# Three buffers for the driven input of a selective scan, and each chunk's gate made by VectorE straight from PSUM

## The reference

```
dA[t]  = exp(delta[t] * A[s])
dBu[t] = (delta[t] * u[t]) * B[t, s]
h[t]   = dA[t] * h[t-1] + dBu[t]              # a scan over the 1024 tokens
y[t]  += h[t] * C[t, s]                       # summed over the 16 states
y = (y + u * D) * silu(z)                     # the gate
attn = y @ Wout.T + bout
```

## Time and profile before

| | |
|---|---|
| median of 3 timed runs | 860.98 us (860.31, 860.98, 864.2) |
| span of the profiled execution, first to last instruction | 858.1 us |
| scan stage in it, first drive to last back | 131.7 to 556.4 us |
| PE, DVE, ACT, POOL busy over the span | 84, 75, 38, 60% |

### The profile page before, as it was taken

The page is one execution under the profiler, slowest core; times in us unless marked ns, Lnnn a source line. Parts: engine busy times, 40 slices in busy tenths (PEclk is TensorE's granted clock), DMA queues, the critical chain, the costliest instruction groups (busy, mean ns, idle before and its releaser), DMA issues.

```text
span 858.1 us, 10173 instructions
## 1 busy us (share of the span) xinstructions
PE 723.1 (84%) x2245; PEld 358.4 (42%) x2246; DVE 646.2 (75%) x880; ACT 328.8 (38%) x364; POOL 512.9 (60%) x266
## 2 busy tenths in 40 slices
PE   6899998778787777878788787996599999999994
PEld 3444343223232222323233232585356666666663
DVE  5388898999999999999999999677444444445442
ACT  1786956455453544444454453111111111111110
POOL 1013234989989899998999999646622222222222
PEclk9999999999999999999999999997599999999998
DMA  9345635766777686586669897297323312322210
GB/s 290 104 138 159 213 140 147 204 171 162 180 175 191 164 199 180 146 207 152 190 174 248 219 223 219 67 386 259 115 74 62 49 33 45 48 42 42 46 29 0
DMA packets 61731, 126.33 MB, mean 147 GB/s; under 512 B 11338, under 2 KB 33290, under 8 KB 61580
## 3 DMA queue, kind: packets, MB, share of 16 engines
q1 hardware_dynamic: 49908, 116.12, 49.5%
q0 software_dynamic: 7152, 8.48, 5.7%
q10 hardware_dynamic: 4648, 1.48, 0.7%
HBM read 98.08 MB, written 24.69 MB: 143 GB/s over the span
## 4 chain that ended last, share of the span: by engine, by line
PE 40%; DVE 28%; issue 13%; POOL 9%; ACT 6%; DMA 1%; DVEq 0%; ACTq 0%; SPq 0%; POOLq 0%
DVE pool L1166 19%; PE PS L740 16%; PE PS L756 8%; POOL pool L1449 6%; PE PS L513 6%; ACT PS L906 5%; PE PS L618 4%; POOL spread L1469 2%; PE PS L748 2%; DVE pool L1154 2%; PE PS L636 2%; DVE pool L1100 1%; DVE pool L1098 1%; PE PS L600 1%; DVE Y L1109 1%
## 5 line engine op out<-in xcount | busy, mean ns | idle before, releaser
L1449 POOL TENSOR_TENSOR pool<-pool,hT 128x1024 f32<-128x1024 f32 x128 | 298.6, 2357 | 24.6 <-PE PS L618 24.6
L618 PE MATMUL PS<-pool,ident 128*128 128x512 f32 x512 | 249.5, 610 | 33.9 <-POOL pool L1449 32.6
L906 ACT ACTIVATE PS<-pool,negA 128x1024 f32 (+1 forms) x128 | 143.1, 1118 | 192.1 <-DVE pool L1166 192.1
L1166 DVE TENSOR_TENSOR_SCAN pool<-PS,pool 128x1024 f32<-128x1024 f32 x96 | 215.7, 2274 | 0.0
L1519 POOL DMA_INDIRECT out<-uT,ptab x39 | 60.5, 1552 | 168.7 <-DVE uT L1395 162.1
L618 PEld LDWEIGHTS PS<-pool,ident 128*128 128x128 f32 x512 | 94.0, 192 | 134.8 <-issue 71.1
L740 PE MATMUL PS<-pool,uT 128*128 (+1 forms) x312 | 145.1, 609 | 0.0
L1154 DVE TENSOR_TENSOR pool<-PS,pool 128x1024 f32<-128x1024 f32 x96 | 117.6, 1225 | 12.5 <-PE PS L600 2.4
L600 PE MATMUL PS<-pool 96*128 96x512 bf16 x256 | 78.8, 390 | 56.2 <-DVE pool L1154 52.9
L1369 DVE TENSOR_TENSOR uT<-uT,PS 128x512 f32<-128x512 f32 x39 | 26.9, 688 | 88.3 <-PE PS L740 85.5
L1469 POOL TENSOR_TENSOR spread<-spread,pool 128x1024 f32<-128x1024 f32 x32 | 75.4, 2357 | 14.9 <-ACT spread L912 14.9
(11 more groups left out here) (174 smaller groups left out, 726.6 us busy)
## 6 DMA issues: line engine op xcount, KB each, us to landing
hT<-C_scratch SPq DMA_DIRECT2D x128, 512.0 KB, 5.3
pool<-in_w SPq DMA_DIRECT2D x16, 512.0 KB
uT<-expert_in_scratch SPq DMA_DIRECT2D x39, 130.5 KB
Y<-Y SPq DMA_DIRECT2D x32, 128.0 KB, 2.4
C_scratch<-Y SPq DMA_DIRECT2D x8, 512.0 KB, 2.6
pool<-du_scratch SPq DMA_DIRECT2D x8, 512.0 KB, 7.2
Y<-in_wo SPq DMA_DIRECT2D x8, 512.0 KB
expert_in_scratch<-zrow SPq DMA_DIRECT2D x16, 130.5 KB, 5.8
```

What stands on the lines that cost most here:

```text
L618: m = pe.matmul(PS[:, 6 + half, :], ident[:, :], prod[:, k % PR, HF * half:HF * half + HF], start=False, stop=k == DS - 1)
L906: act.activation(pair(2 * (k % 2)).unsqueeze(1), delta[:, bass.ds(g2 * 2 + r, 1), :], ACT.Exp, scale=decay[:, bass.ds(g2 * (2 * DS) + n, 1 ...
L1166: dve.tensor_tensor_scan(hst[:, k % HR, :], pair(2 * (k % 2)), driven, 0.0, ALU.mult, ALU.add).then_inc(scan_done, 1)
L1449: gp.tensor_tensor(prod[:, k % PR, :], hst[:, k % HR, :], crep[k % RC], ALU.mult).then_inc(prod_done, 1)
```

## The change

1. A third buffer for `drive`. It is `wz_sb`, the weights of z, which are free once z is made. The buffers are taken in turn by three, and the wait asks for one scan less: for the scans up to n-3, not for the one just before.
2. `leave` moves from ACT to DVE. It is now one multiplication, of the sum in PSUM (banks 6 and 7) by `szT`, written into `uT`: copy and gate in one. It stands behind `drive(4)` and ahead of `scan(3)` of the next chunk. It still signals `yev_done`, on which PE begins the next sum.
3. POOL's `gate_y` goes, and the semaphore `gated` with it; who waited for `gated` now waits for `yev_done`.
4. The last chunk leaves where DVE's last gate stood. Since that now reads the PSUM banks, PE's first gate logits wait for it.
5. As the first chunk has nothing that leaves, DVE's first pass of the loop is written out, and POOL's no longer is.

```
+        dbu_of = [dbu[:, 0, :], dbu[:, 1, :], wz_sb[:, :, :].rearrange("p k n -> p (k n)")]
...
-            sp.wait_ge(gated, NG)
+            sp.wait_ge(yev_done, 1 + NG)
...
-                    pe.wait_ge(gated, CH)
+                    pe.wait_ge(yev_done, 1 + CH)
...
             def logits(t):
                 pe.wait_ge(h2_done, t + 1)
+                if t == 0:
+                    pe.wait_ge(yev_done, 1 + NG)
...
-            def leave(g2, r):
-                act.wait_ge(ysum_done, g2 * (2 * DS) + ((r + 1) * DS + RC))
-                act.sem_inc(passed, 1)
-                act.activation(uT[:, bass.ds(g2 * 2 + r, 1), :], pair(6).unsqueeze(1),
-                               ACT.Copy).then_inc(yev_done, 1)
...
-                        if k == LAG - 1 and not (first and r == 0):
-                            leave(g2 - (1 - r), 1 - r)
...
-                dve.wait_ge(scan_done, g2 * (2 * DS) + (n + 1))
-                dve.tensor_tensor(dbu[:, owned_to(k) % 2, :], pair(4), du[:, r, :], ALU.mult).then_inc(dbu_done, 1)
+                dve.wait_ge(scan_done, g2 * (2 * DS) + n)
+                dve.tensor_tensor(dbu_of[owned_to(k) % 3], pair(4), du[:, r, :], ALU.mult).then_inc(dbu_done, 1)
...
+            def leave(g2, r):
+                chunk = bass.ds(g2 * 2 + r, 1)
+                dve.wait_ge(ysum_done, g2 * (2 * DS) + ((r + 1) * DS + RC))
+                dve.tensor_tensor(uT[:, chunk, :], pair(6).unsqueeze(1), szT[:, chunk, :], ALU.mult).then_inc(yev_done, 1)
...
                     for k in range(1, DS):
                         if k not in SHARED:
                             drive(g2, r, k)
+                        if k == LAG and not (first and r == 0):
+                            leave(g2 - (1 - r), 1 - r)
                         scan(g2, r, k - 1)
...
-            def gate_y(g2, r):
-                chunk = bass.ds(g2 * 2 + r, 1)
-                gp.wait_ge(yev_done, g2 * 2 + (r + 2))
-                gp.sem_inc(passed, 1)
-                gp.tensor_tensor(uT[:, chunk, :], uT[:, chunk, :], szT[:, chunk, :], ALU.mult).then_inc(gated, 1)
...
-                        if k == RC + 2 and not (first and r == 0):
-                            gate_y(g2 - (1 - r), 1 - r)
```

More of the change, by code:

```diff
@@ L246, in adaln_mamba_moe @@
         d_done, zero_rows, xs_zeroed, z_mm, sz_done = (sem(n) for n in ("d_done", "zero_rows", "xs_zeroed", "z_mm", "sz_done"))
-        folded, gated, bout_done = (sem(n) for n in ("folded", "gated", "bout_done"))
+        folded, bout_done = (sem(n) for n in ("folded", "bout_done"))
         regated = sem("regated")
@@ L631, in outward_y @@
                 if t == NTB:
-                    pe.wait_ge(gated, CH * NB)
+                    pe.wait_ge(yev_done, 1 + CH * NB)
                 if t >= 6:
@@ L955, in _ @@
                 decays_of(g2, False)
-            leave(NG // 2 - 1, 1)
             def take_h2(t):
@@ L1162, in scan @@
                 else:
-                    driven = dbu[:, owned_to(k) % 2, :]
+                    driven = dbu_of[owned_to(k) % 3]
                     dve.wait_ge(dbu_done, g2 * (2 * OWN) + (r * OWN + owned_to(k) + 2))
@@ L1167, in scan, with driven_of @@
                                        ALU.mult, ALU.add).then_inc(scan_done, 1)
-            def driven_of(g2, last):
+            def leave(g2, r):
+                chunk = bass.ds(g2 * 2 + r, 1)
+                dve.wait_ge(ysum_done, g2 * (2 * DS) + ((r + 1) * DS + RC))
+                dve.tensor_tensor(uT[:, chunk, :], pair(6).unsqueeze(1), szT[:, chunk, :], ALU.mult).then_inc(yev_done, 1)
+            def driven_of(g2, first, last):
                 for r in range(2):
@@ L1179, in _ @@
             drive(0, 0, 0)
-            with dve.Fori(0, NG // 2 - 1) as g2:
-                driven_of(g2, False)
-            driven_of(NG // 2 - 1, True)
+            driven_of(0, True, False)
+            with dve.Fori(1, NG // 2 - 1) as g2:
+                driven_of(g2, False, False)
+            driven_of(NG // 2 - 1, False, True)
             route = [0]
@@ L1285, in place_of, with leave_last @@
                     dve.tensor_copy(ready[:, :], late).then_inc(ready_known, 1)
-            def gate_y(c):
-                dve.wait_ge(yev_done, 1 + c + 1)
-                dve.tensor_tensor(uT[:, c, :], uT[:, c, :], szT[:, c, :], ALU.mult).then_inc(gated, 1)
+            def leave_last():
+                leave(NG // 2 - 1, 1)
             def residual(q):
@@ L1311, in _ @@
             normal_h2(0)
-            gate_y(NG - 1)
+            leave_last()
             for t in (TQ, TQ + 1):
@@ L1449, in weigh, with weighed_of @@
                 gp.tensor_tensor(prod[:, k % PR, :], hst[:, k % HR, :], crep[k % RC], ALU.mult).then_inc(prod_done, 1)
-            def gate_y(g2, r):
-                chunk = bass.ds(g2 * 2 + r, 1)
-                gp.wait_ge(yev_done, g2 * 2 + (r + 2))
-                gp.sem_inc(passed, 1)
-                gp.tensor_tensor(uT[:, chunk, :], uT[:, chunk, :], szT[:, chunk, :], ALU.mult).then_inc(gated, 1)
-            def weighed_of(g2, first):
+            def weighed_of(g2):
                 for r in range(2):
@@ L1471, in _ @@
             gp.sem_inc(ysum_done, RC)
-            weighed_of(0, True)
-            with gp.Fori(1, NG // 2) as g2:
-                weighed_of(g2, False)
+            with gp.Fori(0, NG // 2) as g2:
+                weighed_of(g2)
             def rstd_of(q):
```

## The result

The changed kernel takes 887.95 us (887.02 to 891.52), the kernel before 860.75 us in the runs beside it: ratio 1.0313, 95% interval 1.0282 to 1.0343. It is slower, as forecast, but by 27.2 us and not 12.9, and the time lies above the range. The span of its profiled execution is 884.9 us, 26.8 more than before.

The account below looks back on a forecast made before the run. VectorE (DVE) was taken to bound the scan stage, GpSimd (POOL) nearly full too. Terms -18.2 + 8.0 + 14.7 - 1.0 + 9.1 + 0.3 = +12.9 gave span 871.0, median 873.9 us; range 856 to 885.

Parts of the forecast that it names:

- Third buffer: Scan stage, VectorE: each of 96 drives starts 0.19 us earlier, no longer waiting for the scan just ahead: 18.2 us less.
- Gate on VectorE: Scan stage: seven `leave`s add a step of 1.14 us each to VectorE, 8.0 us more.
- The wait that it makes: Chunk boundaries: `leave` behind drive(4) delays TensorE, so VectorE idles 2.1 us before drive(5), seven times: 14.7 us more.
- GpSimd's part: Scan stage: GpSimd drops seven gates, 16.5 us beside VectorE; only 1.0 us less was counted, bounds 0 and 2.1.
- The clock: Chunk boundaries: TensorE's 3.9 us stop drops its clock at all seven, 1.3 us each: 9.1 us more, bounds 0 and 12.
- The sign: Whole kernel: slower than before, by 12.9 us in the sum; chance of slower beyond the 0.5% no-change band 0.65.
- Behind the scans: After the scan stage: TensorE's first logits wait for VectorE's last gate, 0.3 us more if it reaches the end.
- over 2 us in the experts' stage: Experts' stage: a move in time of more than 2 us there would show the prediction wrong altogether.
- Rival 1: Scan stage: the clock doesn't fall, or falls where nothing waits: 864.8 us, 52.1 us per chunk; chance 0.20.
- Rival 2: Chunk boundaries: the wait doesn't reach VectorE, as front(5) is ready when scan(3) ends: 848.7 us; chance 0.18.
- Rival 3: Scan stage: the third buffer buys nothing, the 0.10 us behind a scan isn't the semaphore: 890.7 us; chance 0.12.

Follow-up runs that it names:

- e6: Changed kernel with `leave` behind drive(3) instead of drive(4), and two drive buffers instead of three: 866.09 us, ratio 1.0058 to the kernel before.
- e4: Changed kernel with `leave` one step earlier on VectorE, behind drive(3) and ahead of scan(2): 848.31 us, ratio 0.9865 to the kernel before.
- e9: e3 plus a matmul of zeros ahead of each back but a chunk's first: 867.29 us on a faster chip, ratio 1.0177 to the kernel before.
- e1: Kernel before with the third buffer alone, copy still on ScalarE and gate on GpSimd: 856.75 us, ratio 0.997.
- e2: Changed kernel with two drive buffers instead of three, so only the gate's move to VectorE: 906.75 us, ratio 1.0556 to the kernel before.
- e3: Changed kernel with TensorE kept busy ahead of each chunk's sum by repeated fronts of states 4 and 5: 874.1 us, ratio 1.0163 to the kernel before.
- e8: e7 plus a matmul of zeros ahead of each back but a chunk's first: 839.48 us on a faster chip, ratio 0.9839 to the kernel before.
- e7: e1 with GpSimd's gate moved from behind the product of state 6 to behind that of state 1: 855.06 us, ratio 0.9948 to the kernel before.
- e10: e4 plus a matmul of zeros ahead of each back but a chunk's first: 842.7 us on a faster chip, ratio 0.9893 to the kernel before.
- e11: Kernel before plus only a matmul of zeros ahead of each back but a chunk's first: 862.75 us, ratio 1.0022.
- e5: Changed kernel with the front of state 5 moved ahead of the chunk's first identity matmul on TensorE: 889.75 us, ratio 1.0326 to the kernel before.

## Why the prediction missed, point by point

- **Third buffer, -18.2 us.** Right: 0.18 us per drive in the timeline, and between e6 and e4 17.8 us by medians or 16.6 by ratios. The sentence of the Trainium skill that spoke against it ("VectorE: DVE Perf Modes", "The DRAIN you can't avoid") does not hold for these instructions: the wait on the scan just ahead did cost. The same section also says that a next instruction that is not held starts earlier, which the prediction passed over and which is what the rows show.
- **Gate on VectorE, 8.0 us.** Right: a step of 1.13 us, seven times.
- **The wait that it makes, 14.7 us.** Right at full clock: 2.0 to 2.12 us in e9. The stop of TensorE was forecast at 3.9 and is 3.84 to 4.30 us, 3.93 at four of the seven boundaries.
- **GpSimd's part, -1.0.** VectorE's waits for GpSimd fell from 2.1 to 0.5 us, so this term was -1.6. Another -1.3 is the wait at the first boundary, whose slow stretch isn't there in the trace of after: that is chance, and no term had it. Together about -3.
- **The clock, 9.1 us: the step that failed.** The fall at all seven boundaries was forecast and came; its size was wrong, and its reach. The prediction took a slow stretch to last 3.4 us at most, since the kernel before had only such, so 1.3 us per boundary with a bound of 12 us in all, and none elsewhere. Each of the seven stretches lasted 6.8 us and lay over the whole chain: the seven waits are 4.06, 4.84, 5.14, 3.96, 4.21, 4.46 and 4.61 us, 31.3 in all, 16.5 over the order's 14.8. The nine stretches of 3.4 us between the boundaries, of which I had none, cost 5.4 us more:

```profile
DVE pool L1147 <- PE PS L601: 37.4, 15, 5.1
```

  37.4 less 31.3 us behind the gates and 0.7 ahead of the first scan leaves 5.4, in seven waits of 0.35 to 0.90 us, each of which ends inside one of these stretches or within 0.9 us behind it. Together 21.9 us in place of 9.1. The sum with it is -18.2 + 7.9 + 14.8 - 3 + 21.9 = +23.4, and the stage grew by 24.2. The prediction tied the clock to the new stop alone. But slow stretches away from any long stop came with the third buffer alone (e1) and with the gate alone (e2), and their cost was left at nothing.
- **The sign.** It rests on the clock too. Without the 21.9 us the stage would be 413.3 us, 2.3 over the kernel before, which the prediction itself counts as no change. e9 agrees: 413.3, with 3.5 for the repeated fronts in chunk 0 and 1.7 for its one slow stretch, is 418.5, measured 418.4. That is closer than it should be, as e9 also has 2.0 us more of short waits for ScalarE and GpSimd.
- **Behind the scans, 0.3 us.** The first logits do wait for the gate, 0.72 us. The part behind the last scan grew by 2.3 us, within what it varies by. The growth lies ahead of the experts: their first matmuls start 3.0 us later after the last scan, and their own stretch is no longer than before, so the sign "over 2 us in the experts' stage" isn't met. A slow stretch of 3.4 us, 18 us behind the last scan, is in this trace and not in those of before and of e4, whose last gate stands in the same place and which has 310.4 us here; that it is the cause is not shown.
- **Rivals.** Rival 1 named the right hinge (the clock) on the wrong side; its distance of 52.1 us per chunk is met in e9, where the clock stays up. Rival 2's condition, front(5) ready when scan(3) ends, is met in e4, and the time comes out at the 848.7 us worked out for it: the condition only needed the gate one step earlier. Rival 3's numbers were the nearest of all, 890.7 us and 55.5 us per chunk (measured 887.95, and 55.6 on average), but that is luck: the drives do start 0.08 us before the scans end, and e6 against e4 prices the buffer. A number alone would have named the wrong cause.
- **The range** ended at 885 because the clock's bound came from the stretches that happened to be in the trace. The cause of the extra time is shown for the boundaries (e3, e9: same order of the gate, other clock, other wait). The 5.4 us between them I put down to the clock because the waits stand at slow stretches and are gone in e9, where these stretches are gone, and by what e8 did to e7.

## What to carry to other kernels

When a hand-over moves to the busiest engine, look at what stands ahead of it there and how long the receiver will stand still: here the same change costs 27 us with the gate behind one product and gains 11 with it ahead. A new stop of TensorE in a chain of latencies is paid twice, once as the wait and once more in the clock, and the second part isn't bounded by the stretches that the trace of before happens to have. Where TensorE has slack and the others wait for it, cheap matmuls that change nothing can be worth more than the edit they accompany (e8 against e7), and nothing at all where it is hardly waited for (e10, e11).

## What the runs showed of the hardware

- The slow stretches of these stages lasted 3.4 us or 6.8 us. At the seven stops of 3.84 to 4.30 us in the changed kernel it was 6.8 us each time, and the clock fell 0.9 to 3.6 us after the stop had begun, before it ended.
- The length of the stop alone doesn't tell which it is. In e2 one of seven stops of 4.05 to 4.14 us has a stretch of 3.4 us; in e5 all seven stops of 2.7 to 3.1 us have 6.8; in e1 one of 6.8 follows a stop of 1.77. In the changed kernel the stretches at 168, 294 and 393 us begin over 12 us behind the last stop of 1.5 us or more.
- A VectorE product that waits on the scan just ahead starts 0.10 us after its end, one that doesn't 0.08 us before it; and the latter is listed as 1.20 us long in place of 1.225.
- The gate's computed address cost VectorE nothing visible: a step of 1.13 us with it (249.92 to 251.05), as at the first boundary, whose address is fixed (1.13).
- The same kernel before had medians of 859.5 to 860.8 us in four groups of runs and 852.8 on one chip. No trace of it was taken there; in the kernels traced there 3.7 to 5.9 us of the difference lie behind the scans.
